# Whole-width state reads, a read shared with GpSimd, and a new timetable for one PSUM bank in a bidirectional selective scan

## The reference, cut to what matters

```python
def mamba(seq, p):                       # 64 channels in, di = 128 inside, 16 states
    x, z = split(seq @ in_w.T)
    x = silu(causal_conv(x, conv_w, conv_b))                    # 4 taps
    dt, Bm, Cm = split(x @ xp_w.T)                              # 4 + 16 + 16
    delta = softplus(dt @ dt_w.T + dt_b)
    # per channel d and state n, along the sequence:
    #   h[t] = exp(delta[t, d] * A[d, n]) * h[t-1] + delta[t, d] * x[t, d] * Bm[t, n]
    #   y[t, d] = sum over n of h[t] * Cm[t, n]
    y = selective_scan(x, delta, A, Bm, Cm, D)                  # + x * D
    return (y * silu(z)) @ out_w.T
xr = 0.5 * (mamba(seq) + flip(mamba(flip(seq))))                # rows, then columns
```

## Time and profile before

| | us |
|---|---|
| median of three runs | 28833.9 |
| the profiled execution, own time | 28818.42 |
| its span | 28816.6 |
| VectorE busy in the span | 26552.6 (92%) |
| GpSimd busy | 24957.4 (87%) |
| TensorE busy | 19154.9 (66%) |
| ScalarE busy | 17102.0 (59%) |
| granted TensorE clock, mean | 0.76 of full |

### The profile page before, as it was taken

How to read it: one execution, slowest core, us unless ns; L and a number is a source line. 1 busy time by engine, 2 the same in 40 slices (tenths; PEclk the granted TensorE clock), 3 DMA queues, 4 the chain that set the end, 5 groups by cost and what they waited for, 6 DMA issues and landing times. The chain is left out here.

```text
span 28816.6 us, 293743 instructions
## 1 busy us (share of the span) xinstructions
PE 19154.9 (66%) x62778; PEld 5633.3 (20%) x62778; DVE 26552.6 (92%) x29715; ACT 17102.0 (59%) x23653; POOL 24957.4 (87%) x10756
## 2 busy tenths in 40 slices
PE   6666666666666666666666666666666666663283
PEld 1111111111111111111111111121111121111141
DVE  8999999999999999999999999999999999997211
ACT  5666666666666666666666666666666666663132
POOL 8999999999999999999999999999999999995000
PEclk7777777777777777777777777777777777776596
DMA  5555555555555555555555555555555555557757
GB/s 184 193 194 194 194 194 195 194 194 194 194 194 194 195 194 194 194 194 196 195 196 195 198 196 194 196 196 196 195 194 194 196 196 197 197 196 186 152 120 177
DMA packets 1896951, 5507.95 MB, mean 191 GB/s; under 512 B 346354, under 2 KB 610306, under 8 KB 1882258
## 3 DMA queue, kind: packets, MB, share of 16 engines
q1 hardware_dynamic: 1894792, 5485.39, 55.4%
HBM read 4678.99 MB, written 805.60 MB: 190 GB/s over the span
## 5 line engine op out<-in xcount | busy, mean ns | idle before, releaser
L760 POOL TENSOR_TENSOR drive<-du_rep,b_rep 128x1024 f32<-128x1024 f32 x8192 | 19131.7, 2357 | 1379.2 <-DVE state L696 1140.3
L696 DVE TENSOR_TENSOR_SCAN decay<-decay,drive 128x512 f32<-128x512 f32 x11264 | 13133.6, 1211 | 306.9 <-issue 147.0
L572 ACT ACTIVATE decay<-delta_rep,a_neg 128x1016 f32<-128x1016 f32 x8192 | 9043.6, 1108 | 2625.9 <-DVE state L696 1716.4
L709 DVE TENSOR_TENSOR read<-decay,c_rep 128x512 f32<-128x512 f32 x11264 | 7122.1, 673 | 0.1
L769 POOL TENSOR_TENSOR read<-state,c_rep 128x1024 f32<-128x1024 f32 x2560 | 6044.5, 2361 | 1.8 <-DVE state L696 1.8
L696 DVE TENSOR_TENSOR_SCAN state<-decay,drive 128x512 f32<-128x512 f32 x5120 | 5951.0, 1202 | 0.0
L435 PE MATMUL y_bank<-read,sel_f 128*32 128x512 f32 x32768 | 4994.6, 738 | 77.9 <-POOL read L769 53.7
L412 PE MATMUL p_bank<-e_one,sel_f 128*128 128x512 f32 x2048 | 1695.3, 922 | 3173.4 <-ACT e_one L555 1829.0
L399 PE MATMUL p_bank<-u,to_dt 128*128 128x512 f32 x2048 | 2120.4, 1138 | 2247.1 <-ACT zs L617 1405.8
L568 ACT COPY decay<-zeros 128x8 f32<-128x8 f32 x5632 | 931.8, 165 | 3699.7 <-DVE read L709 3687.8
L389 PE MATMUL p_bank<-xt,taps 128*128 128x512 f32 x4096 | 2835.7, 829 | 386.9 <-ACT bc L529 383.8
(11 more groups left out here) (90 smaller groups left out, 13922.3 us busy)
## 6 DMA issues: line engine op xcount, KB each, us to landing
du_rep<-du_spread SPq DMA_DIRECT2D x2048, 512.0 KB, 6.3
delta_rep<-delta_spread SPq DMA_DIRECT2D x2048, 512.0 KB, 8.1
b_rep<-bc_spread SPq DMA_DIRECT2D x2048, 512.0 KB, 8.3
c_rep<-bc_spread SPq DMA_DIRECT2D x2048, 512.0 KB, 7.2
du_spread<-e_log SPq DMA_DIRECT2D x512, 512.0 KB, 2.7
delta_spread<-e_one SPq DMA_DIRECT2D x512, 512.0 KB, 3.7
xt<-in_xs SPq DMA_DIRECT2D x1024, 128.0 KB, 3.6
bc_spread<-bc SPq DMA_DIRECT2D x1024, 64.0 KB, 2.1
```

Source lines behind the costliest of these rows:

```text
L572: nc.scalar.activation(inner(place[:, :]), inner(delta_rep[:, j, :]), ACT.Exp, scale=a_neg[s][:, ROW * j + m:ROW * j + m + 1]).then_inc(s_ ...
L696: nc.vector.tensor_tensor_scan(out[:, px(d)][:, ::step], decay[PLACE[h][q]][:, px(d)][:, ::step], drive[:, q % DRIVE_RING, px(d)][:, ::ste ...
L709: nc.vector.tensor_tensor(read[:, q % READ_RING, px(d)], states[:, px(d)], c_rep[:, m, px(d)], ALU.mult).then_inc(s_read_v, 1)
L760: nc.gpsimd.tensor_tensor(drive[:, q % DRIVE_RING, :], du_rep[h][:, j, :], b_rep[:, m, :], ALU.mult).then_inc(s_drive, 1)
```

## The change

Five things change together.

- VectorE reads a state in one instruction of 1024 columns, not in two of 512, and one pair later: the read of pair q-1 stands between the two scans of pair q. The read of the last pair (15) follows its own second scan, and only its FWD half is VectorE's.
- The REV half of pair 15 is scanned into a new SBUF tensor `state_half`, and GpSimd reads it, as an instruction of 512 columns, the last of its step 15.
- The gate moves from after pair 3 to after pair 4.
- The timetable moves earlier: du from after pairs 3 and 7 to 2 and 5, "ds" of ScalarE from 2 and 6 to 2 and 5, "bc" from 8 to 6, "x" from 9 and 10 to 7 and 8, silu from 11 to 9, "dt" from 12 and 13 to 10 and 11, "out" from 15 to 13, and the first two softplus parts from 13 and 14 to 12 and 13.
- The counts of the semaphores follow. The rings of drive, decay, state and read keep their sizes.

```diff
-STEPS = [Step("ds", FWD, 1, 0, 2), Step("ds", REV, 1, 4, 6), Step("bc", 0, 1, 7, 8),
-         Step("x", FWD, 2, 8, 9), Step("x", REV, 2, 9, 10), Step("z", 0, 1, 10, 11),
-         Step("dt", FWD, 2, 11, 12), Step("dt", REV, 2, 12, 13), Step("out", 0, -1, 14, 15)]
-SOFTPLUS = ((13, 0), (14, 1), (14, 2), (15, 3))
-DU = {FWD: 3, REV: 7}
-GATE, UD = 3, 5
+STEPS = [Step("ds", FWD, 1, 0, 2), Step("ds", REV, 1, 3, 5), Step("bc", 0, 1, 6, 6),
+         Step("x", FWD, 2, 6, 7), Step("x", REV, 2, 7, 8), Step("z", 0, 1, 8, 9),
+         Step("dt", FWD, 2, 9, 10), Step("dt", REV, 2, 10, 11), Step("out", 0, -1, 12, 13)]
+SOFTPLUS = ((12, 0), (13, 1), (14, 2), (15, 3))
+DU = {FWD: 2, REV: 5}
+GATE, UD = 4, 5
...
+SHARED = PAIRS - 1
...
# ScalarE, make_decay
-                    at_least(act, s_read_v, 2 * NV * (U - back) + 2 * vector_before(n) + 2)
+                    if n == SHARED:
+                        at_least(act, s_state, 2 * PAIRS * (U - back) + 2 * n + 2)
+                    at_least(act, s_read_v, NV * (U - back) + vector_before(n) + 1)
...
# VectorE, scan (now one direction a call)
+                to = out[:, px(d)]
+                if q == SHARED and d == REV:
+                    at_least(dve, s_read_g, (NG + 1) * U)
+                    to = state_half[:, :]
...
# VectorE, read_state
-                for d in range(2):
-                    dve.wait_ge(s_state, 2 * PAIRS * U + 2 * q + d + 1)
-                    nc.vector.tensor_tensor(read[:, q % READ_RING, px(d)], states[:, px(d)],
-                                            c_rep[:, m, px(d)], ALU.mult).then_inc(s_read_v, 1)
+                part = px(FWD) if q == SHARED else slice(0, WIDE)
+                dve.wait_ge(s_state, 2 * PAIRS * U + 2 * q + (1 if q == SHARED else 2))
+                nc.vector.tensor_tensor(read[:, q % READ_RING, part], decay[PLACE[h][q]][:, part],
+                                        c_rep[:, m, part], ALU.mult).then_inc(s_read_v, 1)
...
# VectorE, body
-                        scan(U, h, q)
-                        if q not in BY_POOL:
+                        scan(U, h, q, FWD)
+                        if q > 0 and q - 1 not in BY_POOL:
+                            read_state(U, h, q - 1)
+                        scan(U, h, q, REV)
+                        if q == PAIRS - 1:
                             read_state(U, h, q)
...
# GpSimd, read_state and body
+                if q == SHARED:
+                    nc.gpsimd.tensor_tensor(read[:, q % READ_RING, px(REV)], state_half[:, :],
+                                            c_rep[:, m, px(REV)], ALU.mult).then_inc(s_read_g, 1)
+                    return
...
+                        if q == SHARED:
+                            read_state(U, h, q)
```

More of the change, by code:

```diff
@@ L80, in pool_before, with reads_by_pool @@
     return sum(1 for n in range(q) if n in BY_POOL)
+def reads_by_pool(q):
+    return pool_before(q) + (q > SHARED)
 class Step:
@@ L177, in scan_stage @@
         state = sb("state", [P, STATE_RING, WIDE])
+        state_half = sb("state_half", [P, HALF])
         read = sb("read", [P, READ_RING, WIDE])
@@ L200, in scan_stage @@
         s_state = sem("state_halves")
-        s_read_v = sem("read_halves_by_vector")
+        s_read_v = sem("read_by_vector")
         s_read_g = sem("read_by_gpsimd")
@@ L426, in sum_row @@
             def sum_row(U, m):
-                pe.wait_ge(s_read_v, 2 * NV * U + 2 * vector_before(ROW * m + ROW))
-                pe.wait_ge(s_read_g, NG * U + pool_before(ROW * m + ROW))
+                pe.wait_ge(s_read_v, NV * U + vector_before(ROW * m + ROW))
+                pe.wait_ge(s_read_g, (NG + 1) * U + reads_by_pool(ROW * m + ROW))
                 if m == 0:
@@ L682, in make_du, with scan @@
                                         ALU.mult).then_inc(s_evac, 1)
-            def scan(U, h, q):
-                dve.wait_ge(s_decay, PAIRS * U + q + 1)
-                dve.wait_ge(s_drive, PAIRS * U + q + 1)
+            def scan(U, h, q, d):
+                if d == FWD:
+                    dve.wait_ge(s_decay, PAIRS * U + q + 1)
+                    dve.wait_ge(s_drive, PAIRS * U + q + 1)
                 n = pool_before(q)
                 if q in BY_POOL:
-                    at_least(dve, s_read_g, NG * U + n - STATE_RING + 1)
+                    last = n - STATE_RING
+                    at_least(dve, s_read_g, (NG + 1) * (U + last // NG) + last % NG + 1)
                     out = state[:, (NG * h + n) % STATE_RING, :]
@@ L693, in scan @@
                     out = decay[PLACE[h][q]][:, :]
-                for d in range(2):
[L695 to L699, removed]
+                step = 1 if d == FWD else -1
+                to = out[:, px(d)]
+                if q == SHARED and d == REV:
+                    at_least(dve, s_read_g, (NG + 1) * U)
+                    to = state_half[:, :]
+                nc.vector.tensor_tensor_scan(to[:, ::step],
+                                             decay[PLACE[h][q]][:, px(d)][:, ::step],
+                                             drive[:, q % DRIVE_RING, px(d)][:, ::step], 0.0,
+                                             ALU.mult, ALU.add).then_inc(s_state, 1)
             def read_state(U, h, q):
                 m, j = group_of(q)
-                states = decay[PLACE[h][q]]
                 dve.wait_ge(s_c[m], 16 * (U + 1))
                 at_least(dve, s_ysum, ROW * U + m - 1)
-                for d in range(2):
-                    dve.wait_ge(s_state, 2 * PAIRS * U + 2 * q + d + 1)
-                    nc.vector.tensor_tensor(read[:, q % READ_RING, px(d)], states[:, px(d)],
-                                            c_rep[:, m, px(d)], ALU.mult).then_inc(s_read_v, 1)
+                part = px(FWD) if q == SHARED else slice(0, WIDE)
+                dve.wait_ge(s_state, 2 * PAIRS * U + 2 * q + (1 if q == SHARED else 2))
+                nc.vector.tensor_tensor(read[:, q % READ_RING, part], decay[PLACE[h][q]][:, part],
+                                        c_rep[:, m, part], ALU.mult).then_inc(s_read_v, 1)
             def gate(U, h, z_taken, projected):
```

## The result

The changed kernel takes **28332.25 us** (median of four runs, 28326.52 to 28341.53) against 28829.89 us: ratio 0.9827, 95% interval 0.981 to 0.9844, 1.7% less, 498 us. The forecast was 28593 us, 241 us less. The direction is right, the time lies in the range, and the gain is a little over twice the one forecast. The profiled execution took 28328.42 us.

What follows compares the result with a forecast made beforehand. VectorE was taken to bound the scan stage: 49.54 work + 0.91 du stall + 0.35 kept waits + 0.03 silu = 50.83 us a unit against 51.30, times 512 = -241 us, so 28,593 us; range 28,110 to 28,880.

Steps and rivals of the forecast that it cites:

- What bounds it: Scan stage: VectorE bounds by its own work, 51.30 us a unit, so a microsecond off each unit is worth 512 us.
- The reads, 1.20 us a unit: VectorE's state reads: ten wide and one half cost 11.84 us against 13.04, saving 1.20 us a unit, between 0.6 and 1.8.
- GpSimd, 49.7 and hidden: GpSimd's drives and reads with the added half: 49.7 us a unit, hidden while VectorE's unit with waits stays above that.
- first rival: Du FWD never stalls: VectorE 49.92 us a unit, GpSimd's 49.7 about the same; -707 us, 28,130 us; chance 0.22.
- The chain to du FWD: Softplus 3, "ds" FWD on TensorE, delta's copy, du: late after h=1 to h=0, stalling VectorE 2.14 us every second unit.
- Its size, 0.91 a unit: VectorE's average stall before du FWD: 2.14 us in five and 0.04 in six of twelve units, 0.91 a unit.
- The kept waits, 0.38: VectorE's waits besides du's: 0.35 us a unit kept of the old 0.56, plus 0.03 for the silu step.
- The wait for delta before pair 2: VectorE's 0.82 us wait for pair 2's decay, behind delta's third load: it goes, as sum_row 2 ends earlier.
- The share at the turns of the loop: VectorE's waits on issue and GpSimd where the unrolled loop turns: 0.32 us a unit, to stay.
- the case without any stall: Range's lower end, 28,110 us: no du stall, 28,130 us; chance 0.22.
- The silu step: ScalarE's silu ahead of pair 12's decay: ready at 36.56, pair 12 starts at 36.60; 0.03 us a unit put.
- rival 2: TensorE's convolutions fall to the low clock, pair 12 late: 30,230 us for both, 29,310 for one; chance 0.09 together.

Runs made afterwards that it cites:

- e5: Changed kernel, but VectorE reads pair 15 whole (1024 columns) and GpSimd has no half read: 28706 us, ratio 0.9951 to the kernel before.
- e9: Changed kernel with each wide read split again into two of 512 columns, back to back in the same place: 28772 us.
- e1: Changed kernel with du FWD after pair 3 instead of after pair 2: 28175 us.
- e7: Changed kernel with five more matmuls, thrown away, on TensorE ahead of the sum of the softplus parts: 28151 us.
- e12: Changed kernel with the old second half of the timetable (silu 11, dt 12 and 13, out 15, softplus 13, 14, 14, 15) and du FWD after pair 3: 28100 us.
- e4: Kernel before with the new timetable only, keeping the old reads (two of 512 columns, no GpSimd half): 28713 us.
- e3: Changed kernel with the old timetable (du after 3 and 7, silu at 11, gate after 3), so the new reads alone: 28796 us.
- e10: e3 with du REV after pair 6 instead of 7: 28802 us.

## Why the prediction was wrong in size, step by step

- **What bounds it**: right. VectorE's work and waits set the unit in the changed kernel. e5 and e9, which add 0.64 and 0.60 of VectorE's work, cost 374 and 440 us.
- **The reads, 1.20 us a unit**: right; 50.74 fell to 49.51. e9 puts the width at 0.60 of it. The estimate from the formula of the Trainium skill ("VectorE: DVE Perf Modes", the section on the TRN2 errata), 1.6 for ten reads, is not borne out as a saving; the starts in the trace were the better guide.
- **GpSimd, 49.7 and hidden**: it is 49.88, and in the changed kernel still mostly hidden. It bounds as soon as du's wait is gone: e1, e7 and e12 end at 50.05, 49.95 and 49.88, with 49.88, 49.88 and 49.84 of GpSimd's work. The prediction's first rival had 28130 us for that case, e7 has 28151.
- **The chain to du FWD**: right in each link. Softplus 3 at +2.67 (forecast 2.7), du at +10.08 (10.0), every second unit, next to none in the others.
- **Its size, 0.91 a unit: this step failed.** It is 0.61. I took the sum's 6.68 us for a constant, from three units that agreed. It is 6.7 in one tile and 5.6 in the next, at the same idle ahead of it, because the clock rises earlier in the one. The mean wait is 253.1/192 = 1.32, not 2.14. That is 0.30 x 512 = 154 us. The three units stood side by side, and the trace of the kernel before had the warning already: 76 of its 410 sums from 3000 to 24000 us took less than 6.2 us, this one 5.1, with two of the four pairs fast:

```profile
8885.90 2.08 PE L412 MATMUL p_bank<-e_one,sel_f 128*128 128x512 f32 x2 [3.17 <-ACT e_one L555]
8887.77 1.58 PE L412 MATMUL p_bank<-e_abs,sel_f 128*128 128x512 f32 x2
8889.19 1.02 PE L412 MATMUL p_bank<-e_log,sel_f 128*128 128x512 f32 x2
8890.05 1.02 PE L412 MATMUL p_bank<-vpos,sel_f 128*128 128x512 f32 x2
```

- **The kept waits, 0.38: also too large.** They are 0.21, 87 us. The wait for delta before pair 2 all but went, as said. The share at the turns of the loop, which were to stay, fell from 0.32 (issue and drives) to 0.17 as well. Why is open; in e4 such waits come to 0.37. In e12 they come to 0.04, but there the wait has another name: all waits before pairs 0 to 2 of the units behind a turn make 0.20 in e12, 0.19 in the changed kernel, 0.38 in e4 and 0.35 before. So it isn't a constant either.
- The two make 0.30 + 0.17 = 0.47 a unit, 241 us, the work 0.03 more (15 us), and the forecast of -241 becomes -498, to within two microseconds. That the two missed parts together equal the forecast is chance. That the measured time lies inside the range owes something to the range's width: its lower end is the case without any stall.
- **The silu step**: right, 0.02 a unit before pair 12. The slow convolutions of rival 2 came, but seldom: 17 of 834 in the changed kernel took some 3.8 us, and VectorE waited before pair 12 in the same 17 places, each time 0.59 us and not the 1.4 that the rival had for one of them. TensorE, then VectorE:

```profile
18077.68 3.78 PE L399 MATMUL p_bank<-xt,taps 128*128 128x512 f32 x4 [1.02 <-ACT u L530]
...
18088.70 1.23 DVE L714 TENSOR_TENSOR_SCAN decay<-decay,drive 128x512 f32<-128x512 f32 x1 [0.59 <-ACT decay L584]
```

- The other convolutions take 2.00 us, or 2.43 where the clock changes within them. In e3 and e10 one of two is slow in every unit, as for the most part in the kernel before.

Not settled: why the clock rises early in 122 of 209 such units of the changed kernel and in only 46 of 205 of e9, and what sets the waits at the turn of the loop.

## What to carry to other kernels

Cost an edit of an engine's timetable as a chain, with every wait between its links, and in the engine's program order: e10 failed because a copy stood behind decays that waited. A duration at the low TensorE clock is no constant of the instruction: look at it in units far apart, not in neighbours, and take both ends for the range. When two engines stand at 99% of a stage, the gain of the first is cut at the work of the second: read that off before adding up.

## What the runs showed of the hardware

- The same eight matmuls took 3.63 us at a granted clock of 1.00, and 5.6 or 6.7 us where it began at 0.50. Added, useless matmuls ahead of them shortened the kernel by 181 us (e7 against the changed kernel), since the sum was on the path and TensorE was not.
- A VectorE instruction that needs the result of the one directly before it starts 0.14 us later than one that doesn't (1.26 against 1.12 us after a scan; 1.25 in the median of the 411 such reads of e5).
- TensorE's clock can fall in the middle of work. In the case shown of a slow convolution the granted clock was 1.00 until 18075.6 and 0.50 from there to 18081.4. It fell inside the first convolution, which came after 1.93 us of idle time and took 2.43 us; before that idle time TensorE had worked for 4 us at 1.00. The second, 1.02 us after the first, took 3.78.
